# Macaron block on one core: one list of steps for the whole run, inputs read in place, first stack issued from three queues, scalar-engine copies one place earlier

## The reference

```
x = x + 0.5 * ffn(layernorm(x))
x = x + attn(layernorm(x))            # no softmax: (q k^T) v, 8 heads
x = x + 0.5 * ffn(layernorm(x))

ffn(x): q, k, v = x@Wq, x@Wk, x@Wv in 16 heads of 16
        scores = q k^T / sqrt(256);  attn = softmax over the last axis (q for each k)
        z = l2norm((attn^T v) @ Wo);  z = l2norm(z @ Wff);  gelu(z)
```

## Time and profile before

| | |
|---|---|
| median of 3 runs | 3022.5 us (3019.59 to 3023.07) |
| profiled execution | 3021.01 us, span 3019.2 us |
| mean granted TensorE clock | 0.983 |
| DVE busy | 2805.7 us (93%) |
| ACT busy | 2734.7 us (91%) |
| PE busy | 2728.0 us (90%) |
| POOL busy | 897.4 us (30%) |

### The profile page before, as it was taken

How to read it: one execution, slowest core, us unless ns; L and a number is a source line. 1 busy time by engine, 2 the same in 40 slices (tenths; PEclk the granted TensorE clock), 3 DMA queues, 4 the chain that set the end, 5 groups by cost and what they waited for, 6 DMA issues and landing times.

```text
span 3019.2 us, 88294 instructions
## 1 busy us (share of the span) xinstructions
PE 2728.0 (90%) x36160; PEld 1083.0 (36%) x36160; DVE 2805.7 (93%) x5659; ACT 2734.7 (91%) x5028; POOL 897.4 (30%) x1195
## 2 busy tenths in 40 slices
PE   5989998999989999899998998988989898898987
PEld 2323343334433334343343333333323333332333
DVE  4999999999999999999999999999999999999996
ACT  2999898998999989999898989999999999999997
POOL 3332323323233232331323323232331323233232
PEclk8999999999999999999999999999999999999999
DMA  8223341233412334123331233423223342323332
GB/s 224 54 45 66 57 100 33 52 74 57 90 40 52 77 57 86 42 51 79 58 83 40 52 83 71 85 49 73 54 61 79 71 85 51 73 53 62 76 71 57
DMA packets 155254, 205.53 MB, mean 68 GB/s; under 512 B 34529, under 2 KB 88289, under 8 KB 154722
## 3 DMA queue, kind: packets, MB, share of 16 engines
q1 hardware_dynamic: 154594, 199.37, 31.9%
q0 software_dynamic: 256, 0.52, 0.1%
HBM read 46.66 MB, written 25.17 MB: 24 GB/s over the span
## 4 chain that ended last, share of the span: by engine, by line
PE 32%; DVE 29%; SPq 17%; issue 8%; ACT 8%; POOL 4%; DMA 2%; POOLq 0%; ACTq 0%; DVEq 0%
DVE exp_ring L656 24%; SPq L374 17%; PE ring L770 11%; PE ring L833 9%; PE o_acc L847 9%; ACT exp_ring L580 5%; PE ring L892 2%; DMA kq_stack<-kq_parts 1%; POOL kq_rest L361 1%; POOL kq_parts L365 1%; DVE w_xn L726 1%; ACT w_xn L592 1%; POOL kq_parts L359 1%; POOL kq_parts L363 1%; PE ring L869 1%
## 5 line engine op out<-in xcount | busy, mean ns | idle before, releaser
L580 ACT ACTIVATE exp_ring<-exp_ring,neg_max 128x1024 f32<-128x1024 f32 x2048 | 2344.0, 1146 | 217.1 <-DVE exp_ring L656 209.3
L656 DVE TENSOR_SCALAR_CACHE_REDUCE exp_ring<-ring 128x1024 f32<-128x1024 f32 x2048 | 2407.2, 1216 | 134.7 <-PE ring L833 128.5
L833 PE MATMUL ring<-kq_stack 128*32 128x512 bf16 x16384 | 1155.8, 384 | 161.2 <-DVE exp_ring L656 58.4
L847 PE MATMUL o_acc<-exp_ring,v_scaled 128*32 128x512 f32 x8224 | 1078.9, 600 | 66.0 <-POOL v_scaled L513 41.9
L833 PEld LDWEIGHTS ring<-kq_stack 128*32 128x32 bf16 x16384 | 400.9, 96 | 1089.1 <-issue 338.8
L513 POOL TENSOR_TENSOR v_scaled<-v_now,exp_rsums 128x64 f32<-128x64 f32 x513 | 153.3, 299 | 1708.0 <-DVE exp_rsums L671 1697.8
L580 ACT ACTIVATION_READ_ACCUMULATOR exp_ring<-exp_ring,neg_max 128x1 f32 x2048 | 381.9, 186 | 0.0
L847 PEld LDWEIGHTS o_acc<-exp_ring,v_scaled 128*32 128x32 f32 x8224 | 249.1, 111 | 296.6 <-POOL v_scaled L513 72.1
L770 PE MATMUL ring<-ffn_wo_wowff,o_T 128*32 128x256 f32 x4352 | 258.9, 380 | 3.5 <-DVE exp_ring L656 2.1
L770 PE MATMUL ring<-xn_T,ffn_wqkv 128*32 128x512 f32 x2112 | 256.9, 606 | 3.0 <-DVE exp_ring L656 1.9
L359 POOL TENSOR_TENSOR kq_parts<-kq_stage,zero 128x512 bf16<-128x512 f32 x130 | 143.2, 1101 | 251.3 <-ACT kq_stage L610 149.6
(11 more groups left out here) (102 smaller groups left out, 1298.3 us busy)
## 6 DMA issues: line engine op xcount, KB each, us to landing
kq_stack<-kq_parts SPq DMA_DIRECT2D x2072, 64.0 KB, 2.4
x_post<-x_slots SPq DMA_DIRECT2D x17, 1024.0 KB, 5.7
x_prep<-x_slots SPq DMA_DIRECT2D x16, 1024.0 KB, 8.4
x_slots<-x_post SPq DMA_DIRECT2D x8, 1024.0 KB, 5.6
out<-x_post SPq DMA_DIRECT2D x8, 1024.0 KB, 4.7
x_prep<-in_L_attn_x SPq DMA_DIRECT2D x1, 1024.0 KB, 5.6
exp_ring<-in_L_attn_w_qkv SPq DMA_DIRECT2D x1, 512.0 KB
kq_stack<-kq_parts POOLq DMA_DIRECT2D x8, 64.0 KB, 3.9
```

Source lines behind the costliest of these rows:

```text
L580: nc.scalar.activation(e, e, ACT.Exp, bias=negmax[:, i % NM:i % NM + 1], scale=-1.0, accum_out=sums[:, g % EG, c:c + 1]).then_inc(exp_done, 1)
L656: nc.vector.tensor_scalar(E[:, (g % EG) * HQ + c, :].rearrange("p (b n) -> p b n", b=NB), ps, -1.0, None, ALU.mult, ALU.min, accum_out=neg ...
L833: last = mm(ps[k:k + COLS, n, :], kq[:, 0, c, j * P + k:j * P + k + COLS], kq[:, 1, c, n * BANK:(n + 1) * BANK], start=True, stop=True)
L847: last = mm(O[32 * c:32 * c + 32, n, :], vsc[a][:, g % EG, c, :], E[:, (g % EG) * HQ + c, n * BANK:(n + 1) * BANK], start=(a == 0 and j == ...
```

## The change

The four lists become one list of steps over the whole run, in which a step stands at phase x 128 + place, and each engine sorts it for itself. What changes with it:

- A step exists only when its phase does. In phase 0 nothing is finished (no u, norms, gelu, x1, nor the accumulator copy of the phase -1), in phase 15 nothing is prepared (no ln, xn, xt, qk 0 to 3, v 0 to 2).
- A place over 128 is taken from the table of the phase to which the step belongs, not from the one in which it falls. This differs at two borders only: the last `recip`, `av` and `z` of phase 0 now use the plain places (5.1, 9.1, 7.7) in linear phase 1, and those of phase 8 the linear ones in phase 9.
- `LEAD`: on ACT the steps qk, u, xt, xt2 and gram stand one place, that is one tile, earlier than on the other engines.
- The input is read where it lies; x_slots holds only the results of the first two layers.
- The first stack (phase 0, quarter 0): 16 transfers from SP, 8 from ACT, 8 from POOL (before: 24 from SP, 8 from POOL). The weight preparation moves into the list, and on DVE ahead of the splits.
- `x1` in four pieces of 512 values per partition instead of two of 1024; the gelu function is `Gelu_apprx_tanh`; POOL also writes the negated mean (128x8) after each rstd, which nothing reads with these tables.
- The memory set of exp_ring and the 16 matmuls of zeros on it (L808) that stood for the accumulator of phase -1 are gone.

```diff
-            placed.append((place % TILES, len(placed), step))
...
+    LEAD = {"sp": {},
+            "pe": {},
+            "act": {"qk": 1.0, "u": 1.0, "xt": 1.0, "xt2": 1.0, "gram": 1.0},
+            "dve": {},
+            "pool": {}}
...
+    for p in range(-1, PHASES + 1):
+        at, places = p * TILES, table(p)
...
+                elif kind in PREP and i >= AHEAD.get(kind, NT):
+                    if 0 <= p < PHASES:
+                        put(at + place, kind, p, i)
+                elif kind in PREP or kind in ("load_xp", "stack0"):
+                    if p + 1 < PHASES:
+                        put(at + place, kind, p + 1, i)
+                elif kind in ("stack1", "stack2", "stack3"):
+                    if 0 <= p < PHASES:
+                        put(at + place, kind, p, i)
+                elif p >= 1:
+                    put(at + place, kind, p - 1, i)
+
+    def order(engine):
+        placed = []
+        for n, (place, step) in enumerate(steps):
+            kind = step[0]
+            parts, gap = PARTS.get(kind, 1), GAP.get(kind, 0)
+            place -= LEAD[engine].get(kind, 0)
...
-            sp.dma_start(xs[0:B], x_in).then_inc(x_copied, 16)
...
+                    sp.dma_start(xp[:], tokens(x_in[p] if p < B else xs[p - B])).then_inc(xp_loaded, 16)
...
+                    wait_splits(sp, p, q // 2)
+                    if q >= 2:
+                        sp.wait_ge(filled["tile"], nth("pe", "tile", p, (q - 1) * QT - 1))
+                    elif p >= 1:
+                        sp.wait_ge(filled["tile"], nth("pe", "tile", p - 1, (q + 3) * QT - 1))
+                    stack_quarter(sp, q, range(HQ - 2) if (p, q) == (0, 0) else range(HQ))
...
+                elif kind == "stack0" and p == 0:
+                    wait_splits(act, 0, 0)
+                    stack_quarter(nc.scalar, 0, range(HQ - 2, HQ - 1))
...
+                    nc.gpsimd.tensor_tensor(negm[:], zero[:, 0:1].to_broadcast([P, NT]), mv[:, :, 0],
+                                            ALU.subtract).then_inc(rstd_ready, 1)
...
-                            nc.scalar.activation(wb[:, t, 0:D], wb[:, t, 0:D], ACT.Gelu,
+                        last = nc.scalar.activation(wb[:, c, 0:D], wb[:, c, 0:D], ACT.Gelu_apprx_tanh,
```

1227 lines of the change are left out of this document (646 added, 581 removed).

## The result

| | median | runs | profiled execution |
|---|---|---|---|
| before | 3023.7 us | 13 (3019.6 to 3032.9) | 3021.0 us, span 3019.2 |
| changed | 3039.7 us | 13 (3028.3 to 3047.8) | 3042.2 us, span 3040.3 |

The ratio is 1.0045, with a 95% interval of 1.0035 to 1.0055: the change makes the kernel slower by 0.45%, where I had forecast 2979 us and 1.5% faster. Every ratio in the experiments is to runs of the kernel before that were measured beside that run, whose medians lie between 3023.9 and 3026.8 us.

The account below looks back on a forecast made before the run. No single engine bounds the kernel: loops through SP in plain phases, elsewhere PSUM slots held by ACT. Terms -6 - 3 - 16 + 1.5 - 12 - 7 - 0.5 = -43 took 3021.0 to 2978, median 2979 us; range 2948 to 3002.

Parts of the forecast that it names:

- Loop B: Plain phases, place 41.7 to about tile 80: SP's quarter 2 transfers, POOL's qk 0 split, v_scaled, then PE's av set the time.
- loop A: Plain phases: quarter 1 starts after PE's last tile of the phase before; issue, landing and split bring a 1.54 us gap at tile 18.
- -2.0 each: Lead in plain phases 9 to 14: loop B starts 1.15 us earlier, later gaps give about 0.9; -12 us in all.
- If in loop B v_scaled is not what holds: Rival: half of all idle time could go, 4 us a plain phase, 3.5 a linear one; 2943 us, chance 0.2.
- ACT waits: Rival: ACT, running in order, waits at copies moved ahead of exponentials, making row sums late; 3058 us at 0.15 a copy, chance 0.05.
- the 1.54 stay: Plain phases, tile 18: loop A starts from PE's last tile and does not move, so its 1.54 us gap remains.
- about 0.2 us of DVE a phase: Cost of four x1 pieces against two, hidden by loop B or PE's wait; uncovered, 3 us in all.
- -16: Lead in linear phases: earlier copies remove DVE gaps at tile 39 and at qk copies of tiles 77 to 87, -2.0 us each.
- First stack: -6: Start: SP issues 16 transfers instead of 24 at 0.69 us each, ACT 8 beside it; gain 6.2 to 6.9, taken as 6.
- 16 x 1.04: First stack, if the queues made each other half as slow again: 16.6 us of issue, gain only 1.4 us.
- Phase 0 and phase 15: Phases with less work: -3 us in phase 0, most savings hidden by loop B; -7 in phase 15.
- The border and the tail: Border from plain to linear: PE waits for the later z, +1.5 us once; tail: last x1 piece half the size, -0.5.

Follow-up runs that it names:

- f3: The kernel before with only POOL's plain-phase splits of qk 0 and qk 4 moved just behind the next recip: 3004.2 us, ratio 0.9929.
- e4: The changed kernel with POOL's splits of qk 0 and qk 4 moved behind the next v_scaled in phase 0 and plain phases: 2981.5 us, ratio 0.9855.
- e3: The changed kernel with the store of out back at its old place behind quarter 3: 3032.8 us, ratio 1.0021.
- h1: The changed kernel without ACT's lead and with the store of out back behind quarter 3: 3027.7 us, ratio 1.0008.
- e1: The changed kernel with ACT's lead taken back to zero, all else kept: 3043.4 us, ratio 1.0059.
- g3: f4 with the store of out late again, between quarter 0 and the load of x_prep: 2959.1 us, ratio 0.9784.
- f2: f1 with ACT's lead taken back to zero: 2992.6 us, ratio 0.9889.
- f1: The changed kernel with e4's moved POOL splits, x1 in two pieces and the store of out behind quarter 3: 2962.6 us, ratio 0.9792.
- h2: f4 with linear phases' splits of qk 0 and qk 4 just behind the next v_scaled, order of splits kept: 2984.1 us, ratio 0.9865.
- f4: f1 with x1 as one instruction instead of two pieces: 2959.9 us, ratio 0.9782.
- e2: The changed kernel with x1 in two pieces instead of four, lead kept: 3021.8 us, ratio 0.9991.

## Why the prediction was wrong, by its own steps

- **Loop B and loop A.** The links I read rightly: the split waits for the last transfer, v_scaled stands behind the split, PE behind v_scaled. The step that failed is "From the last split of the phase (place 41.7) to about tile 80 the time is set by this, whatever DVE has to do", and with it the "-2.0 each" of the plain phases. In the kernel before, this loop hardly bound at tile 82: DVE's gap there was 0.2 us, and f3, which frees v_scaled, left the third quarters at 45.0. The lead takes away the gap at tile 76 (1.0 to 1.4 us before), DVE comes to the wait for v_scaled sooner, and only now does it bind (gap 2.7 at tile 82, 1.0 without the lead). I priced the loop as a fixed time and did not ask what stands on POOL behind the split that it ends in. Freeing v_scaled is worth 21 us in the kernel before (f3) and 58 in the changed one (e4): 37 us of what the change was to bring were held at this one place.
- **From -12 to +17.3 in the plain phases.** This is not the lead's doing: in the profiles it gives 1.1 to 1.3 us a phase, 6 to 8 us, where I had 12. The late store costs 3.1 to 3.4 a phase, 19 to 20 us in these profiles, which exaggerate it: by the medians it is 7 us (e3) and 16 (h1 against e1). The 0.8 us a phase by which h1 is above the kernel before is not explained; what else differs there (the pieces of x1, the gelu, the negated mean) was not tried singly in plain phases. With v_scaled first, the store costs nothing (g3) and the lead gives 3.5 a phase (f2 against f1).
- **The rivals.** None covers the outcome. The one at 0.2 ("If in loop B v_scaled is not what holds") was right of tile 82 in the kernel before, but in the changed kernel v_scaled does hold, and the idle time stayed. The slower one, "ACT waits", did not come about: ACT waits 4.3 us for PE ahead of its qk copies in all plain phases together, and 13.7 in the whole run (4.3 before).
- **The clock.** It is in no term. Around the gaps of 2.7 to 3.7 us at tile 82 (phases 10, 12, 13, 14) PE was granted 1.2 GHz for 6.8 us each time, and DVE waited again at tiles 84 and 86: 1.4 us a phase in all, against 0.2 in e4. Of the gap at tile 82 itself a part is the clock's too: in phase 12 it is 2.83 us from the start of the av to DVE's next tile, and 1.54 in h2's phase 5 at full clock. An estimate from these rows is some 2.2 us a phase, 13 us over six phases; it was not tested by itself. A low clock need not cost anything: g3 has 3.4 us of it in each third quarter, and these take 43.4 us against 43.3 in f4. At tile 18 gaps of 2.6 to 3.3 us brought none.
- **The store of `out`.** The prediction has no term for its move from behind quarter 3 to behind quarter 0, and says of loop A "the 1.54 stay". The gap at tile 18 went from 1.9 to 3.8 us, and 2.1 with the store early.
- **Four x1 pieces: "about 0.2 us of DVE a phase".** In each linear phase x1 lasts 2.8 us longer and the second quarter 2.4; two pieces give back 2.0 of the phase and one piece 2.7. That is 19 us over eight phases against some 7 that the lead gives in their first and fourth quarters, and so +11.6 where I had -16. I had expected PE's wait to hide the pieces; it did not. I had counted the starts of instructions and not asked what POOL does beside them. The Trainium skill, page SBUF — State Buffer, section SBUF: two separate sides, has the rule that I did not use: of a VectorE instruction with two inputs in SBUF and a GpSimd instruction that reads SBUF, the one that starts first gets their shared port pair for its whole instruction. x1 is such an instruction, the split too, and the traces agree: x1 takes 5.14 us in four pieces and 2.28 in one.
- **The lead.** Linear phases: the first and the fourth quarter fell by 0.7 and 0.2 us, and the gap at tile 39 went, but x1's collision took more. -0.8 a phase is what it is worth with x1 in two pieces (f2 against f1), not -2.0, since it still makes x1 last 3.20 us in place of 2.35. In plain phases, with v_scaled first, it is -3.5, not -2.0. That the lead's 30 us in f2 come close to my 16 + 12 is chance: the two parts are 7 and 21.
- **First stack: -6.** The step that failed is the price of a transfer: I took SP's settled 0.69 us, as if it cost the same on each queue and beside any other. With ACT and POOL issuing too it took SP 0.98 us, near the "16 x 1.04" that I had named and put aside. The third queue gave some 1.9 us; the rest of the 3.3 is that SP's first transfer came 1.1 us earlier, at a time that varies by 2 us between traces (35.1 to 37.2 in the variants of the changed kernel). The page that I had named, Trainium Kernel Development and Optimization of the Trainium skill, section Key Constraints, says that several issuers save issue time only. The traces agree, and even of the issue time little was saved: SP's fell from 17.99 to 15.68 us, not to 11.1.
- **Phase 0 and phase 15.** -0.6 for phase 0 where I had -3: it too has the two stalls. "Were loop B not there, they would give about 7" was borne out: with POOL mended on both sides, phase 0 takes 174.4 in the old kernel and 168.2 in the new. Phase 15 gave 5 of 7. The wait of 4.4 us for quarter 2's transfers at tile 64 is new there: with less work on DVE the loop through SP does bind in this phase, where I had written only that "loop B ends with quarter 2". The border and the tail are what I had said.

So there was as much to be had as I had said: with POOL's order mended the old kernel takes 3004.2 and the new one (two pieces, store early) 2962.6, a difference of 42. That this is near my 43 is luck, since hardly a term has the size that I gave it. The change as it stood lost it at two places: 37 us at v_scaled behind the waiting split, and 18 (e2) at the port that x1 and the split share. What stays open is why h1's median fell by only 16 us against e1's: the profiled executions differ by 21 and the first quarters of phases 10 to 14 by 17, and h1's runs spread from 3022 to 3041. Open too is why quarter 1 was issued in 24.1 us in e1 and in 22.9 in the changed kernel, with the same transfers.

The best kernel is the changed one with v_scaled ahead of the waiting splits, the early store and x1 in one instruction: 2959.9 us, 2.2% below the kernel before. Some 21 us of that come from moving POOL's splits, which the kernel before could have had as well. (Its two neighbours, with two queues at the start or the late store, can't be told from it.)

## What to carry to other kernels

Where an instruction waits for a transfer, look at what stands *behind* it in the same engine's queue. If others need that at once, move it ahead of the wait, before looking for time anywhere upstream. Do so only where there is a wait: in the linear phases, where there was none, the move cost 24 us. Time gained just ahead of such a stop comes back in it, and a stop that did not bind before can bind once the gaps ahead of it are gone. And when an instruction is cut in pieces, ask what another engine that shares its port will do between them: here x1 in four pieces lasted 5.14 us beside POOL's split, and 2.49 without it.

## What the runs showed of the hardware

- DVE's x1 (two inputs in SBUF) and POOL's split instructions take turns at the borders of instructions, and who starts first holds: in f4 x1 starts 0.2 us earlier and POOL's first instruction takes 2.98 us; in h2 the split starts 0.15 us earlier and x1 takes 3.03. The whole x1, by its pieces and by how long after its start POOL's split began: four pieces and 0.2 us, 5.14 us; four pieces and 1.26 us, 3.33; two pieces and 0.2 us, 3.20; two and 1.26 us, 2.35; one, 2.28. POOL's first instruction took 1.38, 1.52, 1.92, 1.99 and 2.98 us in the same order, against 1.04 alone. DVE's tile instruction, which reads PSUM, shows nothing of it: 1.22 us beside a split or not.
- Around a standstill of 3.7 us at tile 82 of phase 12 PE was granted 0.50 of its clock for 6.8 us (from 2420.3 on), and 16 tile matmuls took 1.93 us in place of 1.05. In the kernel before, behind a wait of 0.9 us at the same place, it was not (1.05), but at the end of a wait of 2.8 us at tile 76 it was, for 3.4 us (1.90).
- The 32 transfers of quarter 1 were issued in 22.8 to 24.1 us (means of phases 10 to 14) in the six traces where SP's queue has a store and a load of 1 MB just ahead of them, and in 21.8 to 22.6 in the eight variants of the changed kernel where it has the load alone. Why is not shown.
- A 64 KB transfer issued by ACT beside SP and POOL took ACT 1.29 us (10.29 for 8) and SP 0.98 (15.68 for 16), while SP beside POOL alone took 0.73 (17.49 for 24). POOL's took 0.53 in both (4.20 for 8).
